# Two attention stages: where the fourth unit's scores and maximum stand among the next block's query work

## The chip, the cores and the metric

The program runs on one core of a Trainium2 chip. The metric is the device time of one execution in microseconds (us): 1284.89 us is the median of three runs, which went from 1282.65 to 1289.13.

## What is computed

A gated two-layer block over x of shape 16 x 256 x 256 with a context of 16 x 77 x 256. Cut to its core:

```python
def xattn(q, kv, Wq, Wk, Wv, Wp):                 # 16 heads of 16
    scores = einsum('bhnd,bhmd->bhnm', Q, K) / sqrt(16)
    attn = softmax(where(mask, -inf, scores))
    return merge_heads(einsum('bhnm,bhmd->bhnd', attn, V)) @ Wp

x = x + tanh(g_xattn[0]) * L0_xattn(layernorm(x), ctx, ctx, mask)
x = x + tanh(g_ffn[0])   * mixture_top2_of_8_experts_plus_shared(layernorm(x))
x = x + tanh(g_xattn[1]) * L1_xattn_block(layernorm(x), ctx)   # attention, norm, ffn, norm
x = x + tanh(g_ffn[1])   * L1_ffn(layernorm(x))
```

The change is in the code that both attentions share.

## The kernel before

The program runs as a line of stages: the first attention (about 15 to 275 us of the profiled execution), the mixture (to about 630), the second attention (to about 890), and two feed-forward stages. Each attention goes over 16 blocks (b), one for each batch of 256 rows by 256 columns. What is done for one block is called a turn. Each engine has its own function that writes out its instructions in a fixed order: `attention_on_tensor` (PE), `attention_on_vector` (DVE), `attention_on_scalar` (ACT) and `attention_on_gpsimd` (POOL). No scheduler reorders anything; the order of the calls in each function's `body` is the order on the engine, and semaphores tie the engines together. In the first attention all but the first and the last turns run in a hardware loop that holds two turns.

Scores, softmax and the weighing of values of one block go in four units j = 0 to 3: two groups of 8 heads, times two tiles of 128 queries. For each unit PE makes the scores (`score`, L782, 6 matmuls of 320 columns, into the half j % 2 of the score banks, over a mask that ACT has laid there), DVE takes the row maximum (`score_max`, L430) and subtracts it (`less_max`, L437), ACT takes the exponential (L653 and L654), PE transposes the result (`transpose_prob`, L791), ACT copies it out (L670), PE weighs the values (`weigh_values`, L801 and L803), and DVE divides by the row sum (`normalise`, L445 and L447).

Beside block b's four units the same turn prepares block b + 1 and finishes block b - 1:

- the next block's keys and values (`keys_values` on PE, L746 and L731 to L733), rounded by ACT (L622), with the rest taken by DVE (`keys`, L408) and the value tails (L418);
- the next block's normalised rows, transposed (L758), rounded by ACT (L640), their residue by DVE (`x_residue`, L393), then the queries (`queries`, 12 matmuls at L731 to L733), rounded by ACT (`q_rounded`, L645), and their residue by DVE (`q_residue`, L400);
- the last block's output, transposed (`transpose_o`, L812), rounded by ACT (`o_rounded`, L674), its residue by DVE (`o_residue`, L453), its product with the output weights (`project`) and its sum with x (`residual`).

Every product is made of rounded parts and residues: three matmuls for each pair. Matmuls of `score` of the next block wait for `q_split` (the query residue), those of `queries` for `x_split` (the x residue), and `transpose_o` of the last block waits for `o_done` of unit 0 of this block, because both use one PSUM bank. `score_max` waits for `scores_ps`, `less_max` for the maximum and for an earlier exponential.

The second attention takes its rows from the mixture through indexed loads that POOL issues (L947) in its own fixed order, and there the first turn also holds the statistics of the third block (`late_rows`: `ln_stats` L370 and `ln_aggregate` L378). POOL's inverse deviation of that block (`inverse_std`, L934 and L936) waits for them, and two indexed loads for the fourth block stand behind it.

## Time and profile before

| what | value |
|---|---|
| median of three runs | 1284.89 us (1282.65 to 1289.13) |
| the profiled execution | 1282.42 us |
| its span, first to last instruction | 1280.6 us |
| mean granted TensorE clock | 0.979 |
| PE busy, share of the span | 1189.9 us, 93% |
| DVE busy | 1002.2 us, 78% |
| ACT busy | 771.1 us, 60% |
| POOL busy | 659.3 us, 51% |
| chain that ended last | PE 70%, DVE 12%, issue 7%, ACT 5%, POOL 4% |

How to read it: busy times are sums over the span, the chain is what was waited for, from the last instruction back. PE leads both. The lines of the score, the products and the transposes of the attentions (L782, L731 to L733, L791, L803) are among the first of the chain. Shares of the whole span are means over stages with different limits, so what decides is read in the turns of the attentions.

### The profile page before, as it was taken

To read this page: it belongs to the slowest core of one execution; us is meant where nothing else is said; L and a number is where in the kernel's file an instruction comes from. 1 tells how busy PE (TensorE), PEld (TensorE's weight loads), DVE (VectorE), ACT (ScalarE), POOL (GpSimd) and SP (SyncE) were. 2 spreads that over 40 slices of the span, in tenths; PEclk is the share of its full clock that TensorE was granted. 3 is DMA by queue.
4 is the path that set the end of the run, shared out by engine and by line. 5 is a ranking of instruction groups with operands and counts; after the bars stand their busy time and mean duration, and the time that the engine had idled before them with its cause. 6 is when DMAs were issued, how large, how long until landed. Compare 5 with 4: busy or idle time off the path is not lost.

```text
span 1280.6 us, 27101 instructions
## 1 busy us (share of the span) xinstructions
PE 1189.9 (93%) x9168; PEld 1097.9 (86%) x9169; DVE 1002.2 (78%) x2107; ACT 771.1 (60%) x1487; POOL 659.3 (51%) x755
## 2 busy tenths in 40 slices
PE   5999999989888999999799999999999998799997
PEld 4888888879877999999788888888799997678877
DVE  5788888867787676666688888887987876888886
ACT  4677776758645555555477777766444445466663
POOL 4333333323203655554687777631554654578786
PEclk9899999989999999999899999999999999899999
DMA  3121211123200433334543333302000000000000
GB/s 100 52 53 52 53 52 52 39 65 102 80 2 26 114 105 103 108 101 108 116 70 64 64 65 60 60 23 94 23 2 0 0 0 1 1 26 25 25 25 34
DMA packets 72317, 68.66 MB, mean 54 GB/s; under 512 B 26624, under 2 KB 64256, under 8 KB 72000
## 3 DMA queue, kind: packets, MB, share of 16 engines
q1 hardware_dynamic: 58112, 47.60, 12.7%
q0 software_dynamic: 12576, 18.62, 7.7%
q10 hardware_dynamic: 1568, 1.68, 0.5%
q8 instruction: 32, 0.52, 0.2%
q14 instruction: 29, 0.24, 0.1%
HBM read 44.00 MB, written 18.61 MB: 49 GB/s over the span
## 4 chain that ended last, share of the span: by engine, by line
PE 70%; DVE 12%; issue 7%; ACT 5%; POOL 4%; DMA 1%; SPq 0%; ACTq 0%; DVEq 0%; POOLq 0%
PE PSUM L731 12%; PE PSUM L733 12%; PE PSUM L732 11%; PE PSUM L782 6%; PE PSUM L803 6%; PE PSUM L791 4%; PE PSUM L746 2%; PE PSUM L801 2%; PE PSUM L2667 2%; PE PSUM L2668 2%; PE PSUM L758 1%; PE PSUM L2659 1%; PE PSUM L2648 1%; PE PSUM L2647 1%; PE PSUM L1855 1%
## 5 line engine op out<-in xcount | busy, mean ns | idle before, releaser
L2099 POOL TENSOR_TENSOR s_f_h_lo<-s_f_h,s_f_h_hi 128x512 fp32r<-128x512 f32 x64 | 90.0, 1414 | 106.9 <-ACT s_f_h_hi L2049 106.4
L1278 POOL DMA_INDIRECT s_m_tile_x<-normed_x,s_tokens x78 | 95.5, 1224 | 77.0 <-DVE s_tokens L1569 55.5
L803 PEld LDWEIGHTS PSUM<-s_a_v_diagonal,s_a_prob_t 128*128 128x128 f32 x1024 | 126.8, 193 | 0.0
L803 PE MATMUL PSUM<-s_a_v_diagonal,s_a_prob_t 128*128 128x36 f32 x1024 | 125.9, 269 | 0.0
L947 POOL DMA_INDIRECT s_x<-sorted_y,s_slots x60 | 95.4, 1590 | 47.9 <-DMA s_x<-sorted_y,s_slots 31.3
L430 DVE TENSOR_REDUCE s_a_row_max<-PSUM 128x8 f32<-128x640 f32 x128 | 104.3, 815 | 12.8 <-PE PSUM L782 9.6
L670 ACT ACTIVATE s_a_prob_t<-PSUM 128x640 f32<-128x640 f32 x128 | 89.4, 699 | 32.9 <-PE PSUM L791 31.2
L437 DVE TENSOR_TENSOR s_a_less<-PSUM,s_a_row_max 128x640 f32<-128x640 f32 x128 | 105.0, 820 | 3.6 <-issue 0.2
L653 ACT ACTIVATE s_a_prob<-s_a_less 128x512 f32<-128x512 f32 x128 | 80.5, 629 | 45.2 <-DVE s_a_less L437 44.8
L782 PE MATMUL PSUM<-s_a_kd,s_a_q_hi 64*128 64x320 f32 x512 | 90.9, 360 | 15.2 <-DVE s_a_q_lo L400 13.4
L2043 ACT ACTIVATE s_f_h<-PSUM,s_cols 128x512 f32<-128x512 f32 x64 | 44.0, 688 | 90.2 <-PE PSUM L733 82.1
L791 PE MATMUL PSUM<-s_ident,s_a_prob 128*128 128x128 f32 x640 | 94.4, 279 | 2.9 <-ACT s_a_prob L654 2.9
L959 POOL TENSOR_TENSOR s_x<-s_x,s_a_bias 128x512 f32 (+1 forms) x16 | 20.3, 1271 | 145.6 <-DVE s_a_xn L387 135.0
L731 PE MATMUL PSUM<-s_m_x_hi,s_m_up_w 128*128 128x256 f32 x312 | 91.2, 292 | 1.2 <-issue 1.0
L663 ACT ACTIVATE PSUM<-s_a_mask 128x640 f32<-128x640 f32 (+1 forms) x128 | 89.4, 700 | 0.0
L2496 POOL TENSOR_TENSOR s_t_gh<-s_t_h,s_t_g 128x1024 f32<-128x1024 f32 x32 | 78.2, 2442 | 21.0 <-ACT s_t_h L2457 21.0
L733 PE MATMUL PSUM<-s_m_x_lo,s_m_up_w 128*128 128x256 f32 x312 | 88.1, 282 | 0.0
L732 PE MATMUL PSUM<-s_m_x_hi,s_m_up_w 128*128 128x256 f32 x312 | 88.0, 282 | 0.0
L791 PEld LDWEIGHTS PSUM<-s_ident,s_a_prob 128*128 128x128 f32 x640 | 76.6, 151 | 3.7 <-issue 3.7
L782 PEld LDWEIGHTS PSUM<-s_a_kd,s_a_q_hi 64*128 64x128 f32 x512 | 48.7, 185 | 31.7 <-issue 17.0
L731 PE MATMUL PSUM<-s_ffn_hi,s_f_h_hi 128*128 128x256 f32 x256 | 73.2, 286 | 2.0 <-POOL s_f_h_lo L2099 2.0
L733 PE MATMUL PSUM<-s_ffn_lo,s_f_h_hi 128*128 128x256 f32 x256 | 72.3, 282 | 0.0
(314 smaller groups left out, 4283.6 us busy)
## 6 DMA issues: line engine op xcount, KB each, us to landing
sorted_y<-s_m_tile_y SPq DMA_DIRECT2D x39, 256.0 KB
s_a_kd<-s_a_k_parts SPq DMA_DIRECT2D x256, 20.0 KB
s_x<-x SPq DMA_DIRECT2D x16, 256.0 KB, 2.8
s_a_ctx<-ctx SPq DMA_DIRECT2D x32, 128.0 KB
s_moe_raw<-moe_w SPq DMA_DIRECT2D x16, 256.0 KB
normed_x<-s_m_xn SPq DMA_DIRECT2D x16, 256.0 KB, 3.3
y<-s_x SPq DMA_DIRECT2D x16, 256.0 KB, 2.1
s_late_raw<-moe_w SPq DMA_DIRECT2D x11, 256.0 KB, 3.0
```

The costliest lines, as they stand in the source:

```text
L430: dve.tensor_reduce(mx, s, AX.X, ALU.max).then_inc(a.max_done, 1)
L437: dve.tensor_tensor(a.prob[j % 2][:].rearrange("p (c h) n -> p c h n", c=2), s, mx.unsqueeze(3).broadcast_to([P, 2, HPC // 2, CTXP]), ALU. ...
L663: act.activation(a.scores[:, j % 2, :, 0:HPC // 2 * CTXP].rearrange("p c (h n) -> p c h n", n=CTXP), mask.unsqueeze(1).broadcast_to([P, 2, ...
L731: pe.matmul(ps, lh, rh, start=start and i == 0, stop=False, skip_group_check=not start)
L732: pe.matmul(ps, ll, rh, start=False, stop=False, skip_group_check=not start)
L733: last = pe.matmul(ps, lh, rl, start=False, stop=stop and i == n - 1, skip_group_check=not start)
L782: last = pe.matmul(ps, queries[i][rows, m, qt * P:(qt + 1) * P], keys[i][rows, m], start=False, stop=i == 2, skip_group_check=True)
L791: last = pe.transpose(a.prob_t_ps[:, c, :], a.pairs[j % 2][:, c, :], ident[:])
L803: last = pe.matmul(a.o_ps[:, 2 * c:2 * c + 2, :], a.prob_t[j % 2][:, c, :], v[:, j // BT, 0, 2 * c:2 * c + 2], start=False, stop=c == PC - ...
L947: last = pool.indirect_dma_start(x[:, tile, :], None, d["sorted_y"], row, compute_op=ALU.add)
L1278: pool.indirect_dma_start(m.tile_x[n % 2][:, t, :], None, d["normed_x"], bass.IndirectOffsetOnAxis(ap=tokens[:, BT * n + t:BT * n + t + 1] ...
L2099: pool.tensor_tensor(f.h_lo[m % 4][:], f.h[m % 4][:], f.h_hi[m % 4][:].bitcast(F32), ALU.subtract).then_inc(f.h_split, 1)
```

## The change

On PE, the matmuls of `score(b, 3)` stood ahead of `transpose_o` of the last block and the `queries` of the next one; they now stand behind both. On DVE, `q_residue` of the next block stood behind `score_max(b, 3)` (and, in the first turn of the second attention, behind the third block's statistics); it now stands ahead of them. ACT, POOL and SyncE keep their instructions and their order.

```diff
@@ attention_on_vector, body
                 if behind:
                     o_residue(b.last())
+                if ahead:
+                    q_residue(b.next())
                 score_max(b, 3)
                 if late_rows:
                     ln_stats(second.next())
                     ln_aggregate(second.next())
-                if ahead:
-                    q_residue(b.next())
                 less_max(b, 3)
@@ attention_on_tensor, body
                 weigh_values(b, 0)
                 transpose_prob(b, 1)
-                score(b, 3)
                 if behind:
                     transpose_o(b.last(), 1)
                 if ahead:
                     queries(b.next())
+                score(b, 3)
                 transpose_prob(b, 2)
```

On PE, in the second turn of the loop, before: the transposes of unit 1 are the first row, then the register work and the three rows of unit 3's scores, the transposes of the last block's output, and the first three of twelve rows of the queries.

```order
L791 MATMUL PSUM<-s_ident,s_a_prob 128x128 x5
L775 REGISTER_ALU
L782 MATMUL PSUM<-s_a_kd,s_a_q_hi 128x320 x2
L782 MATMUL PSUM<-s_a_kd,s_a_q_lo 128x320 x2
L782 MATMUL PSUM<-s_a_kd,s_a_q_hi 128x320 x2
L812 MATMUL PSUM<-s_ident,s_a_o 128x128 x4
L731 MATMUL PSUM<-s_a_x_hi,s_a_w_hi 128x256
L732 MATMUL PSUM<-s_a_x_hi,s_a_w_lo 128x256
L733 MATMUL PSUM<-s_a_x_lo,s_a_w_hi 128x256
```

Now there is nothing between the transposes of unit 1 and those of the output. On PE, the same turn after the change, from the last row of the queries to the first scores of the next block (the last row):

```order
L733 MATMUL PSUM<-s_a_x_lo,s_a_w_hi 128x256
L775 REGISTER_ALU
L782 MATMUL PSUM<-s_a_kd,s_a_q_hi 128x320 x2
L782 MATMUL PSUM<-s_a_kd,s_a_q_lo 128x320 x2
L782 MATMUL PSUM<-s_a_kd,s_a_q_hi 128x320 x2
L791 MATMUL PSUM<-s_ident,s_a_prob 128x128 x5
L801 MATMUL PSUM<-s_a_v_diagonal,s_a_prob_t 128x144
L803 MATMUL PSUM<-s_a_v_diagonal,s_a_prob_t 128x36 x4
L775 ISA
L782 MATMUL PSUM<-s_a_kd,s_a_q_hi 128x320 x2
```

Unit 3's scores now stand between the queries and unit 2's transposes, so they lie among the work that PE does while the queries are rounded and split.

On DVE, in the first turn of the second attention, the difference (x residue first, then the queries' residue `s_a_q_lo`, the maximum, the third block's statistics, and the subtraction):

```order
 L393 TENSOR_TENSOR s_a_x_lo<-PSUM,s_a_x_hi 128x512
+L400 SCALAR_TENSOR_TENSOR s_a_q_lo<-PSUM,s_cols,s_a_q_hi 128x256 x2
 L430 TENSOR_REDUCE s_a_row_max<-PSUM 128x8
 L370 BN_STATS s_a_stats<-s_x 128x6 x2
 L378 BN_AGGR s_a_mv<-s_a_stats 128x2 x2
-L400 SCALAR_TENSOR_TENSOR s_a_q_lo<-PSUM,s_cols,s_a_q_hi 128x256 x2
 L437 TENSOR_TENSOR s_a_less<-PSUM,s_a_row_max 128x640
```

The queries' residue moved ahead of the maximum and of the statistics here; in all other turns with a next block it moved ahead of the maximum alone.

## Rows read from the trace of the kernel before

**Rows 1.** Window, first attention: length, busy of PE, PEld, DVE, ACT, POOL; PEclk; DMA.

```profile
55.50:241.70 186.20, 181.11 (x1562) 166.00 (x1562) 159.80 (x373) 132.38 (x289) 68.55 (x84) 1.00 0.21 54
```

**Rows 2.** Waits of PE, same window: us in total, times, longest us.

```profile
PE PSUM L782 <- DVE s_a_q_lo L400: 5.5, 13, 0.4
```

**Rows 3.** Timeline, PE, end of a turn: start, us, instruction [idle before <-releaser].

```profile
112.74 0.41 PE L782 MATMUL PSUM<-s_a_kd,s_a_q_hi 64*128 64x320 f32 x2
...
113.37 0.66 PE L812 MATMUL PSUM<-s_ident,s_a_o 128*128 128x128 f32 x4
113.79 0.37 PE L731 MATMUL PSUM<-s_a_x_hi,s_a_w_hi 128*128 128x256 f32 x1
...
115.30 0.71 PE L791 MATMUL PSUM<-s_ident,s_a_prob 128*128 128x128 f32 x5
115.84 0.41 PE L801 MATMUL PSUM<-s_a_v_diagonal,s_a_prob_t 128*128 128x144 f32 x2
...
117.48 0.41 PE L782 MATMUL PSUM<-s_a_kd,s_a_q_hi 64*128 64x320 f32 x2 [0.41 <-DVE s_a_q_lo L400]
```

**Rows 4.** Timeline, ACT, the same turn.

```profile
108.43 0.54 ACT L622 ACTIVATE s_a_k_parts<-PSUM,s_cols 128x80 fp32r<-128x80 f32 x2 [1.47 <-PE PSUM L733]
...
115.50 0.84 ACT L645 ACTIVATE s_a_q_hi<-PSUM,s_cols 128x256 fp32r<-128x256 f32 x2 [0.83 <-PE PSUM L733]
...
118.01 0.63 ACT L653 ACTIVATE s_a_prob<-s_a_less 128x512 f32<-128x512 f32 x1 [0.45 <-DVE s_a_less L437]
```

**Rows 5.** Timeline, DVE, the same turn, from one block's first maximum to the next's.

```profile
102.74 0.82 DVE L430 TENSOR_REDUCE s_a_row_max<-PSUM 128x8 f32<-128x640 f32 x1 [0.26 <-PE PSUM L782]
...
106.19 0.29 DVE L447 TENSOR_TENSOR s_a_o<-PSUM,s_a_row_sum 128x128 f32<-128x128 f32 x1
106.56 0.82 DVE L430 TENSOR_REDUCE s_a_row_max<-PSUM 128x8 f32<-128x640 f32 x1
...
108.16 0.74 DVE L370 BATCH_NORM_STATS2 s_a_stats<-s_x 128x6 f32 x2
109.00 0.51 DVE L408 SCALAR_TENSOR_TENSOR s_a_k_parts<-PSUM,s_cols,s_a_k_parts 128x80 fp32r<-128x80 f32 x2
...
112.88 0.68 DVE L393 TENSOR_TENSOR s_a_x_lo<-PSUM,s_a_x_hi 128x512 fp32r<-128x512 f32 x1
...
115.31 0.81 DVE L430 TENSOR_REDUCE s_a_row_max<-PSUM 128x8 f32<-128x640 f32 x1
116.37 0.88 DVE L400 SCALAR_TENSOR_TENSOR s_a_q_lo<-PSUM,s_cols,s_a_q_hi 128x256 fp32r<-128x256 f32 x2 [0.24 <-ACT s_a_q_hi L645]
117.16 0.81 DVE L437 TENSOR_TENSOR s_a_less<-PSUM,s_a_row_max 128x640 f32<-128x640 f32 x1
118.22 0.82 DVE L430 TENSOR_REDUCE s_a_row_max<-PSUM 128x8 f32<-128x640 f32 x1 [0.25 <-PE PSUM L782]
```

**Rows 6.** Timeline, the next turn: x residue on DVE, then the queries on PE.

```profile
128.20 0.68 DVE L393 TENSOR_TENSOR s_a_x_lo<-PSUM,s_a_x_hi 128x512 fp32r<-128x512 f32 x1
...
129.27 0.37 PE L731 MATMUL PSUM<-s_a_x_hi,s_a_w_hi 128*128 128x256 f32 x1
```

**Rows 7.** Timeline, second attention, first two turns: DVE.

```profile
646.90 0.25 DVE L378 BATCH_NORM_AGGREGATE s_a_mv<-s_a_stats 128x2 f32<-128x6 f32 x2
647.93 0.88 DVE L400 SCALAR_TENSOR_TENSOR s_a_q_lo<-PSUM,s_cols,s_a_q_hi 128x256 fp32r<-128x256 f32 x2 [0.79 <-ACT s_a_q_hi L645]
...
654.66 0.74 DVE L370 BATCH_NORM_STATS2 s_a_stats<-s_x 128x6 f32 x2
```

**Rows 8.** Timeline, the same turns: POOL.

```profile
647.22 0.19 POOL L934 TENSOR_TENSOR s_a_var_eps<-s_a_mv,s_eps_tile 128x2 f32<-128x2 f32 x1 [0.18 <-DVE s_a_mv L378]
...
650.34 1.57 POOL L947 DMA_INDIRECT s_x<-sorted_y,s_slots  x1 [0.30 <-issue]
...
659.51 1.54 POOL L947 DMA_INDIRECT s_x<-sorted_y,s_slots  x1 [2.58 <-DMA s_x<-sorted_y,s_slots]
```

**Rows 9.** Timeline, PE, last turn of the first attention.

```profile
269.64 0.48 PE L801 MATMUL PSUM<-s_a_v_diagonal,s_a_prob_t 128*128 128x144 f32 x2 [0.96 <-DVE s_a_o_lo L453]
```

## The prediction, made before the changed kernel was run

> **What bounds the kernel now.** The change touches only the turns of the two attentions, so I read one turn from inside. First the windows: over twelve turns of the first attention PE is busy 181.1 of 186.2 us, DVE 159.8, ACT 132.4, and TensorE runs at its full granted clock of 1.00, the 2.4 GHz level [rows 1]. That says PE, but DVE has only 14% to spare, and a share doesn't say where in the turn its spare time lies. Then the waits of PE in that window: a single one repeats, before the first scores of the next block, for the query residue; 5.5 us in 13 times [rows 2]. Then the timeline of a turn. It lasts 15.48 us, from one block's first maximum at 102.74 to the next one's at 118.22 [rows 5]. Only two stretches of DVE matter. After the x residue it has room: the last block's output residue, the maximum at 115.31 and the wait for the rounded queries lie there. From the next block's first maximum to the end of the x residue (102.74 to 113.56) it stands nearly without a gap [rows 5]. An instruction of DVE here normally begins 0.07 to 0.09 us before the recorded end of the last one (116.37 + 0.88 = 117.25, and the next is at 117.16). Against that, two rows have some spare time ahead of them: the maximum at 106.56 (the last end was 106.48, so 0.17) and the keys at 109.00 (last end 108.90, so 0.18) [rows 5]. So PE waits 0.41 us per turn, and DVE could be 0.35 us later at the keys before it costs anything.
>
> **The change, part 1: the wait before the next scores goes.** The queries start at 113.79, ACT has them at 115.50, DVE at 116.37 until 117.25, and PE's scores of the next block begin at 117.48: 3.69 us after the queries' start [rows 3 to 5]. PE's own work in between takes 3.69 - 0.41 = 3.28. The scores of unit 3 take 0.63 from their start to the next instruction (112.74 to 113.37) [rows 3]. With them inside, PE's own work is 3.91 and longer than the 3.69: the wait is gone, and the next scores come 0.22 after where they stood, counted from the queries' start. I take 0.25, with 0.03 for the second change of shape. What is gained must therefore come from queries that start earlier.
>
> **Part 2: the queries can hardly start earlier.** Without the 0.63 ahead of them PE would be free for the queries at 113.16 instead of 113.79. But they wait for the x residue, and that ends at 112.88 + 0.68 = 113.56 [rows 5], only 0.23 before the queries start now [rows 3]. In the next turn it is 129.27 - 128.88 = 0.39 [rows 6]. The two values alternate, since the loop holds two turns; the mean is 0.31. This much, less one handover between engines, is all that an earlier start can give. No row shows this handover by itself. The bounds: 0.03, from the rounded queries on ACT (end 116.34) to DVE (116.37), and 0.23, from the query residue to PE's scores, which check several semaphores first [rows 3 to 5]. The queries check one. I take 0.08, nearer to the short ones. Gain: 0.31 - 0.08 = 0.23. PE then has a new wait in front of the output's transposes and the queries, together about 0.4 us, in place of the one it had. The transposes themselves wait for unit 0's division, which ends some 0.6 before the x residue does, and take 0.42 [rows 3], so they don't come last.
>
> **Part 3: DVE comes later out of its free stretch.** The maximum used to fill idle time between output residue and query residue (115.31 to 116.12); now it stands between the query residue and the subtraction, where nothing is idle. The subtraction moves from 117.16 to about 118.02 (0.81 for the maximum and 0.05 for its semaphore), and the next block's first maximum from 118.22 to 118.77: 0.55 later. Half of the moved 0.81 is thus paid from the wait of 0.25 that stood there [rows 5]. Of the 0.55, the 0.35 of spare time take up a part, and 0.20 reaches the keys. But the keys also wait for ACT, which waits for PE's product of the keys [rows 4], and PE is 0.25 later (part 1). The later one counts: keys, and all that follows without a gap down to the x residue, are 0.25 later, counted from the queries' start.
>
> **Part 4: the exponential of unit 3.** It follows the subtraction at once (0.04 behind its end) [rows 4, 5] and moves by 0.84, to 118.85, with its end near 119.7. PE's transposes of that unit, behind the scores and the output product, would come at about 119.85 (the next scores at 117.73, their own 0.63, and some 1.5 for the output product, twelve matmuls like the queries' 1.51). The cover is 0.15 wide, with a handover inside it: 0 to 0.07 lost, I take 0.03.
>
> **Sum for a turn:** +0.25 for the x residue - 0.23 for the closer start + 0.03 = +0.05 us. By the bounds it is -0.05 (all handovers short) to +0.20 (0.23 at the queries). With 26 turns of this kind (13 in each attention): +1.3 us, from -1.3 to +5.2. I saw no reason for the granted clock to fall: a wait of 0.4 only changes its place.
>
> **Part 5: the first turn of the second attention.** Here the queries' residue passes the maximum and also the third block's statistics. They lay in DVE's idle time before 647.93, with the aggregate at 646.90. Now DVE waits first for the rounded queries until 647.93; then residue 0.8, maximum 0.75 and the statistics 0.8 follow, and the aggregate starts at about 650.24: 3.3 later [rows 7]. POOL sits directly behind it (it waited 0.18), so all that stands behind on POOL moves too, above all the last indexed load for the fourth block, from 650.34 to 653.7 [rows 8]. The rows of such a load arrive about 2.6 after POOL has issued it, by the wait at 659.51 [rows 8]: near 657.8. DVE's statistics at 654.66 [rows 7] need these rows; keys, value tails and x residue stand behind them. So DVE, and with it the queries, come 2.9 to 3.4 later, and nothing gives it back, since a turn has no spare time. If the rows arrive sooner than I think, at least the subtraction is late, by 1.7 (650.4 for 648.7), and PE waits for its exponential. Bounds +1.7 and +3.4; I take +3.1, since POOL's chain is shown link by link.
>
> **Part 6: the last turns.** Without queries, the output's transposes move up by up to 0.63, and in the last turn PE does wait for their residue, 0.96 us [rows 9]. 0 to 0.6 gained in each attention; I take 0.5, together -1.0.
>
> The first turn of the first attention I cost at nothing: the queries start earlier there, and the subtraction ends where it did. Total: +1.3 + 3.1 - 1.0 = +3.4 us. The profiled execution took 1282.42, of which 1280.6 is span, so it would become 1285.8. It lies 2.5 under the median of the runs; on the median the forecast is 1284.89 + 3.4 = **1288.3 us**.
>
> **Rival 1, faster: the gap of PE is all that counts.** If the x residue ends earlier than I think relative to the queries (say DVE draws together in its dense stretch once it is pushed), each turn loses PE's whole wait, 0.41 and a little for the restart: 26 x 0.45 = -11.7, with + 3.1 - 1.0 that is -9.6: 1275.3. For it: PE is busiest, and this is its one repeated wait [rows 1, 2]. Against it: the 0.23 and 0.39 between x residue and queries [rows 3, 5, 6]. The Trainium skill, page Perfetto Trace Analysis, section Optimization Strategy, says to find the gaps on the most contended engine and to make what they wait for end sooner; followed here without looking at the second engine, it gives this rival's result.
>
> **Rival 2, slower: DVE sets the turn.** The mechanism: the 0.35 of spare time in DVE's dense stretch isn't there for the taking (register work and semaphore checks fill it), so the whole 0.55 reaches the x residue. Then a turn grows by 0.55 - 0.23 + 0.03 = +0.35; 26 x 0.35 = +9.1, with the ends +11.2: 1296.1. It decides from where less than about 0.2 of the spare time can be used. For it: the second maximum and the keys both follow semaphores with work of the sequencer ahead. Against it: both rows lie just behind what they wait for (the keys 0.03 behind ACT's end at 108.97) [rows 4, 5].
>
> **How the numbers follow.** The forecast's case 0.72, slower rival 0.17, faster rival 0.11. 0.5% (6.4 us) is about what a measurement of this kernel tells from no change. The forecast's own span is 26 turns and the ends at their bounds: -1.3 + 1.7 - 1.2 = -0.8 to 5.2 + 3.4 = +8.6, so 1284.1 to 1293.5; its upper end passes 6.4 with a chance of about 0.07. Hence slower 0.24, within 0.65, faster 0.11. The range reaches down to 1281 for the scatter of the runs and up to 1295, which takes in nearly half of the slower rival: about 0.8.
>
> **What would show it.** In the profile after: PE's wait for the query residue before the next scores gone (part 1); a new one of about 0.4 per turn, for unit 0's division or the x residue, before the output's transposes or the queries (part 2); the first maximum of the next block right behind the subtraction, with no wait (part 3); turns of 15.4 to 15.6; in the second attention DVE's statistics waiting for indexed loads near 657 and the queries after them some 3 late (part 5). I am wrong if turns are under 15.3 (rival 1) or over 15.7 (rival 2), or if the second attention starts without the delay.

## The result, and the profile after

The changed kernel took 1292.42 us (median; 1285.74 to 1300.98), the kernel before 1285.88 us beside it (1282.65 to 1292.68). The ratio is 1.0049, with a 95% interval of 1.0034 to 1.0064: 6.3 us slower, from 4.4 to 8.2. The forecast was +3.4 with an own span of -0.8 to +8.6. The change costs time, a little under what I had called the bound of "no change". The profiled executions differ by 6.0 us of span (1280.6 and 1286.6). Three executions of the experiments below (3798, 1478 and 4943 us, one each of e5, e6 and e7) lie far above the others of their kernels, and neither the ratios nor the comparison at the same clock use them.

The steady turn first. The same window as [rows 1] after the change (us; busy of PE, PEld, DVE, ACT, POOL; PEclk; DMA):

```profile
55.50:241.70 186.20, 184.72 (x1562) 165.85 (x1561) 158.35 (x373) 130.88 (x288) 68.43 (x84) 1.00 0.20 54
```

PE shows 3.6 us more busy time, and the turns are no shorter (table below): the waits have changed places. The waits of PE and of its weight loads (PEld) in that window name the new ones (us in total, times, longest):

```profile
PEld PSUM L812 <- DVE s_a_o L447: 4.3, 12, 0.5
...
PEld PSUM L731 <- DVE s_a_x_lo L393: 2.1, 12, 0.2
...
PE PSUM L812 <- DVE s_a_o L447: 1.1, 5, 0.2
```

The wait for the query residue of [rows 2] is gone. In its place the weight loads wait, for the most part without a gap in PE's own matmul rows, whose ends are modelled: for unit 0's division ahead of the output's transposes, and for the x residue ahead of the queries. The timeline of PE at the end of a turn answers to [rows 3]:

```profile
112.25 0.74 PE L791 MATMUL PSUM<-s_ident,s_a_prob 128*128 128x128 f32 x5
113.21 0.66 PE L812 MATMUL PSUM<-s_ident,s_a_o 128*128 128x128 f32 x4 [0.21 <-DVE s_a_o L447]
113.81 0.38 PE L731 MATMUL PSUM<-s_a_x_hi,s_a_w_hi 128*128 128x256 f32 x1
...
115.41 0.42 PE L782 MATMUL PSUM<-s_a_kd,s_a_q_hi 64*128 64x320 f32 x2
...
116.04 0.77 PE L791 MATMUL PSUM<-s_ident,s_a_prob 128*128 128x128 f32 x5
...
117.80 0.41 PE L782 MATMUL PSUM<-s_a_kd,s_a_q_hi 64*128 64x320 f32 x2
```

DVE in the same turn, to be set beside [rows 5], and the exponential of unit 3 on ACT beside [rows 4]:

```profile
113.07 0.68 DVE L393 TENSOR_TENSOR s_a_x_lo<-PSUM,s_a_x_hi 128x512 fp32r<-128x512 f32 x1
114.69 0.69 DVE L453 TENSOR_TENSOR s_a_o_lo<-PSUM,s_a_o_hi 128x512 fp32r<-128x512 f32 x1 [0.94 <-ACT s_a_o_hi L674]
116.39 0.88 DVE L400 SCALAR_TENSOR_TENSOR s_a_q_lo<-PSUM,s_cols,s_a_q_hi 128x256 fp32r<-128x256 f32 x2 [1.00 <-ACT s_a_q_hi L645]
117.18 0.82 DVE L430 TENSOR_REDUCE s_a_row_max<-PSUM 128x8 f32<-128x640 f32 x1
118.03 0.82 DVE L437 TENSOR_TENSOR s_a_less<-PSUM,s_a_row_max 128x640 f32<-128x640 f32 x1
118.77 0.81 DVE L430 TENSOR_REDUCE s_a_row_max<-PSUM 128x8 f32<-128x640 f32 x1
```

```profile
118.89 0.63 ACT L653 ACTIVATE s_a_prob<-s_a_less 128x512 f32<-128x512 f32 x1 [1.31 <-DVE s_a_less L437]
```

The x residue ends at 113.75 and the queries start at 113.81. Between 115.41 and 117.80 PE has no gap, and the first maximum of the next block stands right behind the subtraction. The chain of waits says the same of the whole program: DVE's share doubled (12% before).

```profile
PE 61%; DVE 23%; issue 7%; ACT 5%; POOL 1%; DMA 1%; SPq 1%; ACTq 0%; DVEq 0%; POOLq 0%
```

**Where PE's turn goes.** From PE's timelines I took the starts of PE's steps, and the time from each start to the next, as means over 11 turns of the first attention (queries starting between 70 and 240 us). Most steps are the same to 0.02 in both kernels; these differ:

| from -> to, us | before | after |
|---|---|---|
| unit 1's transposes -> next step | 0.67 (scores 3) | 0.86 (output's transposes) |
| output's transposes -> queries | 0.41 | 0.60 |
| queries -> next step | 1.51 (transposes 2) | 1.60 (scores 3) |
| transposes 2 -> weighing of unit 1 | 0.54 | 0.60 |
| weighing of unit 1 -> next scores | 1.65 | 1.15 |
| output product -> transposes 3 | 1.51 | 1.48 |
| turn, 11 turns | 15.52 | 15.52 |

The wait for the query residue was 0.50 wide by this measure (0.41 by the released row). The new order pays it back: 0.19 before the output's transposes, 0.19 before the queries, and 0.15 because scores and transposes now stand behind other neighbours, less 0.03 at the output product. The sum is zero.

**Where the time went.** By the queries' starts, 13 turns of the first attention took 201.66 before and 201.74 after, and the last eleven turns with next queries of the second attention 171.11 and 172.22, where the last one alone makes 0.33 of the difference. That is +1.2 us for the steady turns. By the same table of steps, 0.07 per turn is added in the second attention: 0.04 of it ahead of unit 3's transposes (1.49 before, 1.51 after, where the first attention has 1.51 and 1.48), the rest in steps of 0.01 to 0.02. The start of the second attention brings +3.5, its last turn +0.5 (21.72 and 22.24 from its last queries to the first products of the feed-forward stage). The last +0.8 falls behind 902, in that stage, where the two kernels have the same instructions: up to about 930 they stay 5.1 apart, and the changed kernel's window from 925 to 930 was granted 0.66, where the kernel before had 1.00.

In the first two turns of the second attention, DVE after the change (against [rows 7]), then POOL (against [rows 8]):

```profile
647.51 0.88 DVE L400 SCALAR_TENSOR_TENSOR s_a_q_lo<-PSUM,s_cols,s_a_q_hi 128x256 fp32r<-128x256 f32 x2 [2.65 <-ACT s_a_q_hi L645]
...
649.81 0.25 DVE L378 BATCH_NORM_AGGREGATE s_a_mv<-s_a_stats 128x2 f32<-128x6 f32 x2
649.98 0.79 DVE L437 TENSOR_TENSOR s_a_less<-PSUM,s_a_row_max 128x640 f32<-128x640 f32 x1
...
657.35 0.74 DVE L370 BATCH_NORM_STATS2 s_a_stats<-s_x 128x6 f32 x2
659.69 0.51 DVE L408 SCALAR_TENSOR_TENSOR s_a_k_parts<-PSUM,s_cols,s_a_k_parts 128x80 fp32r<-128x80 f32 x2 [1.60 <-ACT s_a_k_parts L622]
```

```profile
650.14 0.20 POOL L934 TENSOR_TENSOR s_a_var_eps<-s_a_mv,s_eps_tile 128x2 f32<-128x2 f32 x1 [3.43 <-DVE s_a_mv L378]
...
653.25 1.57 POOL L947 DMA_INDIRECT s_x<-sorted_y,s_slots  x1 [0.31 <-issue]
```

PE in the same place:

```profile
651.76 0.81 PE L791 MATMUL PSUM<-s_ident,s_a_prob 128*128 128x128 f32 x5 [2.13 <-ACT s_a_prob L654]
```

And the windows around it, after the change (the seventh number is the granted TensorE clock):

```profile
645.00:650.00 5.00, 4.64 (x39) 4.00 (x39) 2.46 (x8) 2.21 (x5) 1.63 (x3) 1.00 0.29 62
650.00:655.00 5.00, 3.24 (x19) 3.17 (x21) 3.63 (x10) 3.44 (x7) 4.28 (x5) 0.74 0.18 26
655.00:660.00 5.00, 5.00 (x30) 4.67 (x29) 2.80 (x7) 0.89 (x3) 4.31 (x4) 0.58 0.48 80
660.00:665.00 5.00, 4.91 (x41) 4.13 (x41) 4.00 (x12) 4.41 (x11) 2.30 (x2) 1.00 0.38 54
```

DVE and POOL are late as forecast. But the keys wait 1.60 for ACT and through it for PE: PE had stood still for 2.13 for the exponential of unit 3, and then ran at the 1.2 GHz level for most of 7 us. In the kernel before, the same wait was 0.92, and both windows from 650 to 660 were granted 1.00:

```profile
650.53 0.76 PE L791 MATMUL PSUM<-s_ident,s_a_prob 128*128 128x128 f32 x5 [0.92 <-ACT s_a_prob L654]
```

How much of this belongs to the change the experiments have to say.

**Times at the same clock.** Each run lists its time and its mean granted clock, and the two go together: over 99 runs of the kernel before and 142 of the others, straight lines of one common slope fit with a scatter of 1.8 us, at 0.87 us for each 0.001 of clock. A kernel's runs also differ in clock by themselves (0.968 to 0.983 after the change). So beside each ratio I give the difference at the same clock from that fit; its 95% interval is 0.9 to 1.4 us to either side (1.7 where there are 5 runs). For the change it is +4.2; the other 2 of the 6.3 us go with a lower clock. Two cautions belong to this. The fit takes the kernel before from the 99 runs beside the experiments, because the clocks of its 20 runs beside the changed kernel are not known. And it takes out whatever part of a kernel's effect goes through the clock: the mean clock was 0.9776 in those 99 runs and 0.9744 in the 20 of the changed kernel (standard errors 0.0003 and 0.0009), so a part of the lower clock may well belong to the change.

### The profile page after: what moved, and what is told of

Same layout as the page of the kernel before. It is cut to its first block, busy times and chain, and to the rows that moved or that the text cites. A ratio compares the mean times of both kernels' runs of the same rounds, so it can differ in the third digit from the quotient of the medians.

```text
span 1286.6 us, 27101 instructions
## 1 busy us (share of the span) xinstructions
PE 1200.2 (93%) x9168; PEld 1099.4 (85%) x9169; DVE 999.8 (78%) x2107; ACT 767.5 (60%) x1487; POOL 659.9 (51%) x755
## 4 chain that ended last, share of the span: by engine, by line
PE 61%; DVE 23%; issue 7%; ACT 5%; POOL 1%; DMA 1%; SPq 1%; ACTq 0%; DVEq 0%; POOLq 0%
PE PSUM L731 12%; PE PSUM L733 11%; PE PSUM L732 11%; DVE s_a_row_max L430 4%; PE PSUM L782 3%; PE PSUM L803 3%; DVE s_a_less L437 3%; PE PSUM L791 2%; PE PSUM L2667 2%; PE PSUM L746 2%; PE PSUM L2668 2%; PE PSUM L812 1%; PE PSUM L2659 1%; PE PSUM L2648 1%; PE PSUM L2647 1%
## 5 line engine op out<-in xcount | busy, mean ns | idle before, releaser
L670 ACT ACTIVATE s_a_prob_t<-PSUM 128x640 f32<-128x640 f32 x128 | 89.5, 699 | 17.8 <-PE PSUM L791 17.1
L732 PE MATMUL PSUM<-s_ffn_hi,s_f_h_lo 128*128 128x256 f32 x256 | 72.7, 284 | 0.0
```

Of the source, the lines that this page charges most:

```text
L670: act.activation(a.prob_t[j % 2][:], a.prob_t_ps, ACT.Copy).then_inc(a.pt_done, 1)
L732: pe.matmul(ps, ll, rh, start=False, stop=False, skip_group_check=not start)
```

## The experiments

All values in one place; "turn" is the mean between queries' starts over 12 turns of the first and 10 of the second attention, "2nd turn" that from the first turn's queries to the second's, in the profiled execution.

| kernel | ratio (95%) | at same clock | turn, 1st att. | turn, 2nd att. | 2nd turn, 1st / 2nd att. |
|---|---|---|---|---|---|
| before | 1 | 0 | 15.51 | 15.51 | 16.2 / 14.9 |
| after | 1.0049 (1.0034 to 1.0064) | +4.2 | 15.52 | 15.59 | 16.9 / 19.4 |
| e1 scores alone | 1.0082 (1.0060 to 1.0105) | +8.4 | 15.76 | 15.78 | 16.9 / 22.2 |
| e2 residue alone | 1.0127 (1.0090 to 1.0163) | +12.2 | 15.84 (15.74 without one of 16.94) | 15.75 | 25.1 / 24.6 |
| e3 statistics first | 1.0036 (1.0012 to 1.0061) | +2.7 | 15.52 | 15.58 | 17.1 / 15.6 |
| e4 statistics in gap | 1.0022 (0.9996 to 1.0049) | +1.1 | 15.47 | 15.53 | 16.6 / 16.7 |
| e5 before + statistics | 1.0031 (1.0005 to 1.0057) | +2.3 | 15.61 | 15.59 | 15.8 / 15.1 |
| e6 after + statistics | 1.0117 (1.0082 to 1.0153) | +9.7 | 15.74 | 15.76 | 17.0 / 22.1 |
| e7 split scores | 1.0055 (1.0031 to 1.0078) | +3.7 | 15.49 | 15.51 | 16.9 / 20.2 |
| e8 split, in gap | 1.0034 (1.0007 to 1.0061) | +0.7 | 15.44 | 15.45 | 16.7 / 15.5 |
| e9 x residue first | 0.9990 (0.9963 to 1.0018) | -0.5 | 15.45 | 15.50 | 20.8 / 15.5 |
| e10 same, old order | 1.0016 (0.9997 to 1.0035) | +1.4 | 15.61 | 15.59 | 16.3 / 22.9 |
| e11 division first | 1.0015 (0.9990 to 1.0040) | +2.0 | 15.46 | 15.50 | 16.7 / 16.6 |
| e12 e11 in gap | 1.0054 (1.0036 to 1.0071) | +2.1 | 15.46 | 15.52 | 21.1 / 21.8 |

**My theory** after the result: the turn is a loop through both engines (queries, PE's work, keys product, ACT, keys, DVE's stretch, x residue, queries), and the change has moved PE's wait, not removed it. **The rival**: the change does gain in the turns, and what is lost is lost at the ends of the stages.

### One half of the change at a time

e1 moves only the scores on PE:

```diff
                 transpose_prob(b, 1)
-                score(b, 3)
                 if behind:
                     transpose_o(b.last(), 1)
                 if ahead:
                     queries(b.next())
+                score(b, 3)
```

> Only the TensorE half of the change: unit 3's scores behind the queries, VectorE's order as in the kernel before. Chain theory (with the scores behind the queries a turn is one closed chain through VectorE): the maximum of unit 3 can now start only about 2.35 us after the queries' start and still stands ahead of the query residue, so the residue begins at 3.1 instead of 2.58 and the next scores at 4.2 instead of 3.95. Turns of about 15.78 us (15.53 in the changed kernel, 15.49 before), 26 of them: +7.5 us; the second attention starts 2 to 4 late; the last turns give 0.7 back. In all +9 to +11 us against the kernel before. Rival (TensorE's gap is all that counts): the wait of 0.41 per turn goes and nothing takes its place, -8 to -12 us.

e2 moves only the residue on DVE:

```diff
+                if ahead:
+                    q_residue(b.next())
                 score_max(b, 3)
...
-                if ahead:
-                    q_residue(b.next())
```

> Only the VectorE half: the query residue ahead of unit 3's maximum, TensorE's order as before. Chain theory: TensorE still waits 0.41 us before the next scores, the subtraction of unit 3 ends 0.86 later, so its exponential ends near 0.1 behind the place where TensorE wants to transpose it: 0.2 to 0.25 us more per turn, 26 turns, +5 to +6.5; the second attention starts 3.5 to 4 us late as in the changed kernel; in all +8 to +11 us. Rival (all that is lost is lost in the first turn of the second attention): +3.5 to +4 us and turns of 15.49.

Both halves are worse than the whole. In e1 the turns took 15.77 (expected 15.78), and the time was 10.5 us longer by the ratio (expected 9 to 11): the x residue to queries distance is 0.06 as in the whole change, and PE additionally waits 0.21 for the query residue, which here still stands behind the maximum. In e2 the steady turns took 15.74 and 15.75 (expected 0.2 to 0.25 more than 15.51); the 15.84 of the table holds one turn of 16.94 that began at the lower clock. PE's wait for the query residue stays, and 0.16 comes on top ahead of unit 3's transposes, since the subtraction and its exponential are late. So the rival, by which one half carries a gain, falls. The two halves need each other, and together they come out even. e2 lost more than expected (16 us by the ratio, for 8 to 11). Its profiled execution has the excess in its starts, where its clock stood at the lower level in both attentions:

```profile
50.00:55.00 5.00, 5.00 (x25) 4.36 (x24) 1.75 (x8) 2.77 (x8) 1.11 (x3) 0.50 0.06 12
...
665.00:670.00 5.00, 5.00 (x26) 4.60 (x25) 2.77 (x7) 2.04 (x5) 4.47 (x5) 0.50 0.39 52
```

### The first turn of the second attention

e3 is the changed kernel with the third block's statistics ahead of the queries' residue:

```diff
+                if late_rows:
+                    ln_stats(second.next())
+                    ln_aggregate(second.next())
                 if ahead:
                     q_residue(b.next())
                 score_max(b, 3)
-                if late_rows:
-                    ln_stats(second.next())
-                    ln_aggregate(second.next())
```

> The changed kernel, but in the first turn of the second attention the third block's statistics stand ahead of the query residue again, where they fill idle time. Chain theory: GpSimd's inverse deviation and TensorE's 2.1 us wait for unit 3's exponential go, with the slow clock behind it; 4 to 4.5 us of the changed kernel's 6.3 are gone, so +1.5 to +2.5 us against the kernel before, with turns of 15.53 in both attentions. Rival (each of the 26 turns is 0.24 us longer): nearly nothing changes, +5.5 to +6.5.

The second turn took 15.6 instead of 19.4 and the clock stayed at 1.00 from 640 to 700. The steady turns are unchanged. By the ratio e3 is 1.7 us below the changed kernel (some 3.7 to either side), at the same clock 1.5 (1.3 to either side). That is less than the nearly 4 by which the second turns of the two profiled executions differ, and less than the 4 to 4.5 that I expected; the rival's "nearly nothing" isn't excluded by the ratio. One reason is that PE's wait for the exponential of unit 3 didn't go away, though I had expected that. It fell from 2.13 to 1.34, with 0.92 before the change:

```profile
649.00 0.76 PE L791 MATMUL PSUM<-s_ident,s_a_prob 128*128 128x128 f32 x5 [1.34 <-ACT s_a_prob L654]
```

The rest of these 4 goes with the clock, and the length of this wait alone doesn't decide on the clock. e7 and e8 (below) show this best, with one execution each. There, the same wait, of the same length, stands at the same place:

```profile
651.26 0.76 PE L793 MATMUL PSUM<-s_ident,s_a_prob 128*128 128x128 f32 x5 [1.48 <-ACT s_a_prob L654]
```

```profile
650.85 0.76 PE L793 MATMUL PSUM<-s_ident,s_a_prob 128*128 128x128 f32 x5 [1.48 <-ACT s_a_prob L654]
```

Of the windows from 655 to 660, the first of these fences' kernel (e7) was granted half, the second (e8) all:

```profile
655.00:660.00 5.00, 5.00 (x25) 5.00 (x25) 2.50 (x7) 1.71 (x6) 2.35 (x2) 0.50 0.40 65
```

```profile
655.00:660.00 5.00, 5.00 (x44) 4.31 (x43) 3.98 (x12) 4.29 (x12) 2.53 (x2) 1.00 0.47 72
```

A first fall of the clock is in all 14 profiled executions, the kernel before included, and in both attentions (but for e3's second): the lowest window of 5 us between 30 and 40, and between 620 and 650, was granted 0.50 to 0.66. What differs is a second fall. The second turn of an attention took either 14.9 to 17.1 us or 19.4 to 25.1, the latter each time with further windows granted 0.50 to 0.61. A second fall goes with 4 to 9 us more, as much as the whole change. The length of a wait doesn't decide on it: e10 had no wait of PE over 0.7 in its second turn and was granted 0.50 for 15 us, e9 waited 1.36 for the exponential and stayed at 1.00. What does decide stays open, and with it how often either order brings a second fall.

### What fills DVE's stretch ahead of the keys

e4 is e3 with the statistics of the block after next taken out of the stretch ahead of the keys:

```diff
-                if ahead > 1 and not late_rows:
-                    ln_stats(b.next().next())
...
-                if ahead > 1 and not late_rows:
-                    ln_aggregate(b.next().next())
...
                     x_residue(b.next())
+                if ahead > 1 and not late_rows:
+                    ln_stats(b.next().next())
...
                 less_max(b, 3)
+                if ahead > 1 and not late_rows:
+                    ln_aggregate(b.next().next())
```

> As the last, and the statistics of the block after next moved out of VectorE's dense stretch in all turns: the statistics between x residue and output residue, where VectorE waits 0.94 us for ScalarE, their aggregate behind the subtraction of unit 3. Chain theory: the dense stretch is 0.8 us shorter, the x residue ends before TensorE comes to the queries, TensorE's own work of 15.0 us sets the turn: 15.0 to 15.15, so -9 to -12 us against the kernel before. Rival (TensorE loses the time itself, by restarting after waits or at its own work; VectorE isn't the cause): turns stay near 15.5 and the kernel within 2 us of the one before it in this list.

This missed: -0.05 per turn instead of -0.35 to -0.45, and +1.1 us at the same clock instead of -9 to -12. The row of the keys says why:

```profile
108.56 0.51 DVE L408 SCALAR_TENSOR_TENSOR s_a_k_parts<-PSUM,s_cols,s_a_k_parts 128x80 fp32r<-128x80 f32 x2 [0.57 <-ACT s_a_k_parts L622]
```

Of the 0.74 taken out of DVE, 0.57 came back as waiting for ACT, which waits for PE's keys product. Ahead of the keys DVE and PE stand level; only what lies behind the keys counts. I had taken the whole dense stretch as the bound, against part 3 of my own prediction, where the later of the two counts.

e5 and e6 put one more statistics instruction into the same stretch, in the kernel before and in the changed one:

```diff
+                if twice:
+                    dve.bn_stats(a.stats_spare[:], x[:, bass.ds(BT * b.n, 1), :])
                 for t in range(BT):
                     last = dve.bn_stats(a.stats[:, t, :], x[:, bass.ds(BT * b.n + t, 1), :])
```

> The kernel before, with one more statistics instruction of DVE (half of the pair at L370, into a spare tile) ahead of the statistics in every turn that has them. By the row it adds about 0.33 us per turn to DVE's stretch ahead of the keys, some 26 times. Theory (the stretch has about 0.35 of spare time, as step 3 of the prediction used): 0 to +0.05 per turn, 0 to +1.3 us. Rival (the spare time is not to be used): +0.33 per turn, +8.6 us, and then the second rival of the prediction would have been right in its mechanism.

> The changed kernel with the same added instruction. Theory (after the change DVE reaches the keys with no spare time, since the subtraction of unit 3 and the next maximum moved back by 0.55): +0.25 to +0.33 per turn on the changed kernel's own time, +6.5 to +8.6 us, so about 1.0105 of the kernel before. Rival (the changed kernel's turn is closed by PE alone and DVE still has room): 0 to +0.05 per turn, ratio about 1.005. The two, with the run on the kernel before, say whether the spare time of DVE is what the change has spent.

The turns grew by 0.09 in the kernel before and by 0.20 in the changed one (means of both attentions), and at the same clock the times by 2.3 and 5.5 us, about 26 turns of each. So of 0.33 added the kernel before hides 0.24, the changed one 0.13. Both theories had the direction right and missed the size (expected 0 to 0.05 and 0.25 to 0.33); both rivals fall (0.33 and 0 to 0.05). In both, 0.09 to 0.10 appears in PE's step of weighing unit 0 (1.16 for 1.06). ACT's values wait for the keys, and its copy of unit 0, which this step needs, stands behind them; that path out of the keys I hadn't counted. And the changed kernel still had some room.

### Filling PE's new waits

By the table of PE's steps the new order has two waits of 0.19, and 15.14 of own work. e7 (on e3) and e8 (on e4) leave the first two of unit 3's six score matmuls where they stood before the change, in the first of these waits:

```diff
                 transpose_prob(b, 1)
+                score(b, 3, (0,))
                 if behind:
                     transpose_o(b.last(), 1)
                 if ahead:
                     queries(b.next())
-                score(b, 3)
+                score(b, 3, (1, 2))
```

> The changed kernel with the statistics of the second attention's first turn ahead of the queries' residue (as in the run on them), and unit 3's scores divided: the first two of their six matmuls stand where they stood before the change, in the 0.2 in which PE waits for unit 0's division, the other four behind the queries. PE then reaches the next scores and the keys product 0.25 earlier, counted from the queries' start. Theory (two bounds lie close together: DVE's dense stretch gives 15.53 per turn, the way through PE's keys product 15.48): the turn stays at 15.5, within 1.5 us of the run with the statistics first, ratio 1.002 to 1.005. Rival (the way through PE is the only bound): 0.25 less per turn, -6.5 us, ratio about 0.999.

> The same divided scores, and the statistics moved out of DVE's dense stretch into its idle time behind the x residue (as in the run of that name, whose turns took 15.48). Theory (now DVE has 0.57 of idle time ahead of the keys, and what ends last is the way queries, scores, output product, keys product, ACT's rounding, keys, x residue): 0.25 less, turns of 15.2 to 15.25, 26 x 0.25 = -6.5 us on that run, so a ratio of 0.997 to 0.999, faster than both kernels. Rival (something else holds the turn, such as ACT or the exponential of unit 3, which stays where it is while PE comes 0.25 earlier and waits for it): turns of 15.4 to 15.5, ratio 1.001 to 1.003.

e7 came as expected in its turn (15.49 and 15.51; its ratio is just above the expected 1.005), e8 didn't: its turn is 15.44, not 15.25. PE's window shows hardly any room:

```profile
60.00:240.00 180.00, 180.00 (x1518) 162.06 (x1516) 154.14 (x361) 128.22 (x282) 68.04 (x82) 1.00 0.20 51
```

PE as matmul is busy in all of it. The two new waits are gone (0.67, 0.34 and 0.41 for the three steps up to the queries), but the split itself costs PE time: 0.34 + 0.49 for the two parts where the whole took 0.64, which is 0.19 more. I had booked a reordering of PE as free. A further 0.09 stands between the output product and the weighing behind it (1.53 + 0.59, for 1.48 + 0.55 in the changed kernel, with the same neighbours). There the rival of e8's expectation has a part, for unit 3's exponential ends at 119.27 and its transposes start 0.06 later:

```profile
118.98 0.29 ACT L654 ACTIVATE s_a_prob<-s_a_less 128x128 f32<-128x128 f32 x1
...
119.33 0.76 PE L793 MATMUL PSUM<-s_ident,s_a_prob 128*128 128x128 f32 x5
```

So 15.14 of own work, 0.19 for the split and 0.09 here come to 15.42 of the 15.44.

e9 (on e3) fills nothing and makes DVE ready sooner. It also moves three instructions of ACT:

```diff
@@ DVE
-                less_max(b, 2)
-                normalise(b, 0)
                 if ahead:
                     x_residue(b.next())
+                normalise(b, 0)
+                less_max(b, 2)
@@ ACT
-                mask_laid(b, 3)
                 if ahead:
                     x_rounded(b.next())
-                exponential(b, 2)
+                mask_laid(b, 3)
                 transposed(b, 1)
+                exponential(b, 2)
```

> The changed kernel with the second attention's statistics ahead of the queries' residue (as in the run on them), and in every turn the x residue ahead of unit 0's division and unit 2's subtraction on DVE, with ACT's rounding of x ahead of the mask of unit 3 and its copy of unit 1 ahead of unit 2's exponential. By PE's rows after the change a turn of 15.52 holds two short waits of 0.19: before the output's transposes (unit 0's division) and before the queries (x residue). The rest, 15.14, is PE's own. Theory (the turn is PE's own work plus these two waits, and both waits end with DVE's stretch behind the keys, from which the subtraction of 0.74 is now gone): both waits vanish, turns of 15.15 to 15.25, 26 x 0.3 to 0.37 = -8 to -10 us on the run with the statistics first, ratio 0.995 to 0.998, faster than both kernels. Rival (the exponential of unit 2, now later, delays ACT's rounding of the output and the queries, and PE waits there instead): turns of 15.4 or more, ratio 1.002 or more.

e10 makes the same moves in the kernel before.

> The same moves of x residue, division, subtraction, rounding, mask and copy, but in the kernel before, where unit 3's scores stand ahead of the queries. Theory (there the x residue has 0.31 to spare and PE's turn is 15.02 of its own and 0.5 of waiting for the queries' residue): nothing is gained; unit 3's scores may wait up to 0.15 for their mask, which is laid 0.6 later: 0 to +4 us, ratio 1.000 to 1.003. Rival (an earlier x residue helps whatever stands behind it): -5 us or more.

e9 is the best of the series and not measurably faster than the kernel before (0.9990, 0.9963 to 1.0018; -0.5 at the same clock). Against e3 it gains 0.07 per turn, not 0.3, so its theory missed. The x residue now ends 0.9 before the queries, but the division stands behind it:

```profile
115.37 0.60 ACT L640 ACTIVATE s_a_x_hi<-PSUM 128x512 fp32r<-128x512 f32 x1 [0.43 <-PE PSUM L758]
...
116.00 0.69 DVE L393 TENSOR_TENSOR s_a_x_lo<-PSUM,s_a_x_hi 128x512 fp32r<-128x512 f32 x1 [0.34 <-ACT s_a_x_hi L640]
...
116.61 0.20 DVE L445 RECIPROCAL s_a_row_sum<-PSUM 128x8 f32<-128x8 f32 x1
...
116.84 0.29 DVE L447 TENSOR_TENSOR s_a_o<-PSUM,s_a_row_sum 128x128 f32<-128x128 f32 x1
...
117.19 0.65 PE L812 MATMUL PSUM<-s_ident,s_a_o 128*128 128x128 f32 x4 [0.29 <-DVE s_a_o L447]
```

The wait before the queries went and the one before the output's transposes grew to 0.33. e10's size was as expected: +0.09 per turn, ratio 1.0016. Its mechanism was not. Unit 3's scores don't wait for their mask (0.68 behind unit 1's transposes, for 0.67). Instead, 0.12 is added between unit 2's transposes and the weighing of unit 1, which waits for the last block's output residue. ACT now rounds that output behind unit 2's later exponential, so the residue ends at 116.64 and the weighing starts at 116.79:

```profile
115.95 0.69 DVE L453 TENSOR_TENSOR s_a_o_lo<-PSUM,s_a_o_hi 128x512 fp32r<-128x512 f32 x1 [1.38 <-ACT s_a_o_hi L674]
...
116.79 0.48 PE L801 MATMUL PSUM<-s_a_v_diagonal,s_a_prob_t 128*128 128x144 f32 x2
```

In the old order an earlier x residue buys nothing.

e11 is e9 with the division first (the edit below is against e9). e12 is e11 with the statistics out of the stretch ahead of the keys, as in e4, but behind the output's residue:

```diff
-                if ahead:
-                    x_residue(b.next())
                 normalise(b, 0)
+                if ahead:
+                    x_residue(b.next())
                 less_max(b, 2)
@@ ACT
                 transposed(b, 1)
-                exponential(b, 2)
                 if behind:
                     o_rounded(b.last())
+                exponential(b, 2)
```

> As the run with the x residue first, but unit 0's division stands ahead of the x residue (then unit 2's subtraction), and ACT rounds the output ahead of unit 2's exponential. In that run one wait of PE was left, 0.33 before the output's transposes, for the division, which could only start behind the x residue at 116.61 while PE had unit 0 ready at 116.15. Theory (each 0.1 by which this wait shrinks is taken off the turn): the division starts near 116.25, the transposes' wait goes, the x residue ends near 117.3 and PE waits 0.1 to 0.2 for it instead: turns of 15.25 to 15.35, so -3 to -5 us on that run, ratio 0.995 to 0.997. Rival (the turn is closed elsewhere by then, by DVE's dense stretch ahead of the keys, where the keys follow the statistics without idle time): turns stay at 15.4 or more, ratio 0.998 or more.

> The last kernel, and the statistics of the block after next moved out of DVE's dense stretch into its idle time between the output's residue and the queries' residue, the aggregate behind unit 3's subtraction. Theory (PE's own work and its short waits behind the keys close the turn; the statistics ahead of the keys hardly count, as in the run with the statistics in the gap, where a turn gained 0.05, the aggregate's part behind the keys): 0.05 to 0.15 less per turn than the last kernel, turns of 15.15 to 15.25, ratio 0.993 to 0.996. Rival (the last kernel is held by DVE's stretch ahead of the keys): this one then gains 0.2 or more per turn on it.

Both missed: the turns stay at 15.46 in the first attention, like e9 and close to e8 and e4, where 15.25 to 15.35 and 15.15 to 15.25 were expected. e11's rows show the loop that is left:

```profile
110.91 0.98 PE L803 MATMUL PSUM<-s_a_v_diagonal,s_a_prob_t 128*128 128x36 f32 x8
...
111.72 0.74 PE L791 MATMUL PSUM<-s_ident,s_a_prob 128*128 128x128 f32 x5
111.92 0.21 DVE L445 RECIPROCAL s_a_row_sum<-PSUM 128x8 f32<-128x8 f32 x1 [0.70 <-PE PSUM L803]
...
112.16 0.29 DVE L447 TENSOR_TENSOR s_a_o<-PSUM,s_a_row_sum 128x128 f32<-128x128 f32 x1
...
112.37 0.68 DVE L393 TENSOR_TENSOR s_a_x_lo<-PSUM,s_a_x_hi 128x512 fp32r<-128x512 f32 x1
...
112.51 0.66 PE L812 MATMUL PSUM<-s_ident,s_a_o 128*128 128x128 f32 x4
```

DVE waited 0.70 and starts the division 0.03 after PE's weighing of unit 0 ends (110.91 + 0.98 = 111.89). Division and x residue take 1.13 from there to the x residue's end at 113.05, and the queries start 0.06 later, at 113.11. PE has only unit 1's transposes and the output's to do in that time: 0.67 + 0.41 from 111.72, to 112.80. The 0.31 of waiting can't be removed by DVE's order, since both operations must lie between the weighing and the queries (or the x residue between the rounding of x and the division, as in e9). Before the change unit 3's scores, 0.64, lay in exactly this place. They were the cover. That these 0.31 close the turn is read from the rows; no kernel of the series has both the whole scores as cover and the next scores without their wait.

e12's statistics changed nothing in the turn, so DVE's stretch ahead of the keys doesn't hold e11. Its 5 us above e11 by the ratio go with the clock (0.9731 for 0.9791 in the mean of the runs, and second turns of 21.1 and 21.8 in the profiled execution); at the same clock the two are equal. That both are then 2 us above the kernel before, with turns that are 0.05 shorter in the first attention, stays open.

## Why the prediction was nearly right, step by step

**Part 1** (the wait before the next scores goes, the next scores 0.25 later): right. They stand 3.99 behind the queries' start (117.80 - 113.81), for 3.69 before: +0.30. PE's own work in between is 3.20 by the table (I had 3.28), the scores add 0.63, and the neighbours 0.15 where I had 0.03.

**Part 2** (queries 0.23 earlier relative to the x residue, a new wait of about 0.4): right. The handover was 0.06 everywhere, not 0.08; the mean distance fell from 0.31 to 0.06, by 0.25. The new waits are 0.19 + 0.19. The text was also right that the transposes, waiting for the division, don't come last: the x residue releases the queries. e9 shows that the division's wait counts as soon as the other is gone.

**Part 3** (subtraction at 118.02, first maximum 0.55 later, keys 0.25 later, counted from the queries): right. The subtraction stands at 118.03; the first maximum is 4.96 behind the queries for 4.43 (+0.53); the keys, one turn on, 10.98 for 10.70 (109.19 - 98.21 for 109.00 - 98.30), +0.28.

**Part 4** (exponential at 118.85, 0.03 lost): 118.89, nothing lost in the first attention; from output product to transposes it takes 1.48. In the second attention some 0.04 of the added 0.07 lies here.

**The sum** of the steady turns, +1.3, was +1.2 in the profiled execution: next to nothing in the first attention, 0.08 per turn in the second and 0.33 in its last one. No run isolates why the second is dearer; its table of steps puts half of it ahead of unit 3's transposes.

**Part 5** (start of the second attention +3.1): the size was near (+4.1 at the second turn, +3.5 two turns on), the link that I named as the last was not. DVE's aggregate came at 649.81 (forecast 650.24) and POOL's load at 653.25 (forecast 653.7), but the statistics at 657.35 show no wait for rows. What came last was the link that I had only as the lower bound, PE's wait for the exponential, 2.13 long for 0.92 before, with the 1.2 GHz level behind it. The forecast had no term for the clock. And the size is not all the change's: with DVE's order in that turn undone (e3) the runs give back 1.5 us, not 3 or 4. This term was over-read from a clean chain, and that its 3.1 lies near the profiled 3.5 is luck.

**Part 6** (last turns -1.0): the step that failed in sign. In the first attention the last weighing did come 0.35 earlier (269.29 for 269.64), but the second attention's first queries start at 630.27 for 630.26: the mixture between gave the gain back, in this pair of executions. In the second attention the last turn took 22.24 for 21.72, so +0.5. A gain at the end of a stage is worth something only if the next stage starts on it.

So +3.4 against the profiled +6.0 is: -0.1 in the steady turns, +0.4 in part 5, +1.5 in part 6, and +0.8 of clock in a stage that the change doesn't touch. In the runs, it is 4.2 at the same clock and some 2 of clock. Of the 4.2, the steady turns account for 1.2, the order in the first turn of the second attention for 1.5 (e3), and the last turn for 0.5; about 1 us stays open.

**The rivals.** Rival 1 (all that counts is PE's gap, 1275.3) needed turns under 15.3. No kernel of the series had one; the best was 15.44. The Trainium skill's rule that I set beside it (page Perfetto Trace Analysis, section Optimization Strategy: find the gaps on the most contended engine and make what they wait for end sooner) would have given -10 us in this rival's reading; the gap was closed, two others opened, and the measured result was +6.3. Rival 2 (the spare time of DVE isn't to be used, 1296.1) needed turns over 15.7. The turns after the change took 15.52 and 15.59, and e6 shows that even more work in the stretch than the change puts there is partly hidden.

## What to carry to other kernels

Before a block of work is moved on the busiest engine to fill a wait, ask what it was covering where it stood: here 0.64 of scores hid a division and a residue of the other engine, and taking them away opened waits of 0.38 in exchange for 0.50, with 0.15 more for the new neighbours. Compare two orders by the time from start to start of each step over many turns; this shows waits that sit in weight loads and in the pace of a step, which the waits of the engine itself don't name. And where a kernel's runs scatter with the granted clock, compare them also at the same clock before a difference of a few us is given to a mechanism, and say that this leaves out what the change does to the clock itself.

## What the runs showed of the hardware

- One handover from DVE to PE, from the recorded end of the x residue to the first query matmul, took 0.05 to 0.06 us in every turn in which PE stood ready. The 0.23 that I had as the upper bound was read at scores that wait for three semaphores; no run takes it apart.
- The same scores took 0.64 in one piece and 0.34 + 0.49 in two; the queries took 1.51 before transposes and 1.60 before scores. A reordering of TensorE's steps wasn't free here even with the same matmuls.
- In the second turn of an attention the granted clock fell, for a second time, to the level of 0.50 for 5 to 15 us in some executions and not in others: behind the same wait of 1.48 once and once not, and in another behind no wait over 0.7. Second turns with such a fall took 4 to 9 us more.
